# A value product for both halves of the probabilities at once, with VectorE adding the two results

## The chip, the cores and the metric

The kernel runs on one core of a Trainium2 chip. The metric is the device time of one execution in microseconds; the median of three runs is compared.

## The reference

One transformer layer (attention and experts side by side) on x of 32 sequences of 256 tokens with 128 features, all in float32:

```python
xn = _layernorm(x)
# attention: h = relu(xn @ w1 + b1); m = h @ w2 + b2; q, k, v = projections of m
# each query sees the keys at distance -32..32
weights = softmax(where(valid, q . k_band / sqrt(128), -inf))
att = einsum('bsw,bswd->bsd', weights, v_band)
# experts: 16, the best 8 of each token weighted, and one shared expert
y = sum over e of combine[e] * ((silu(xn @ gate[e].T) * (xn @ up[e].T)) @ down[e].T)
x + att + y + shared(xn)
```

## The kernel before, in words

The 32 sequences are worked through in 16 groups of two (512 tokens). Features lie on the partitions and tokens on the free dimension, so that nearly every operation is 128x512. A group has 17 steps (`STEPS`), one for the shared expert and 16 for the experts. Each engine has its own program that walks the same groups and steps (`program`, `slot`), and the order written there is the order of execution on that engine; semaphores tie the engines together. There is no planner.

Every float32 operand of a product is split in two float32r parts, "hi" (the value rounded) and "lo" (the rest), and a product is three matmuls: hi by hi, hi by lo and lo by hi (`PAIRS3`). So wherever a tensor is fed to TensorE, ScalarE writes its hi part from PSUM or SBUF and VectorE subtracts it to get lo.

In slot s of a group TensorE issues `gate_proj` of step s+1 (L466), attention work of this step (`att_early`), `down` of step s-3 (L486, `LAG`), more attention work (`att_late`) and `up_proj` of step s (L476). The other engines handle an expert step like this: ScalarE makes silu of the gate product (L717), GpSimd multiplies it by the routing weight (L1262), VectorE multiplies the up product with it (h_prod, L1134), ScalarE takes the hi part (h_hi, L725) and VectorE the lo part (h_lo, L1140). VectorE's slot s is: h_prod of step s-1, the attention work of the slot (`att`), h_lo of step s-1. The up products alternate between two PSUM banks, so that `up_proj` of step s waits for h_lo of step s-2.

Attention is spread over the steps. The scores of the two sequences are in `bank[2]` and `bank[1]`; mask and row maximum, exp and normalisation follow, and TensorE transposes the probabilities (L437). Each sequence has two blocks of 128 keys, and a block is seen by 160 queries (`WIN`). The hi part of the transposed probabilities is `p_t[0]` (L712), the lo part `p_t[1]` (L1043). The value product `attend` (L447) runs in slots 13 and 14, sequence by sequence, with the hidden state hid_n as the stationary operand: for each key block three matmuls into `bank[2]`, where both sequences have 256 columns each. The first one of a sequence is 256 columns wide (the columns past 160 hold zeros from a memset, L975) so that it writes all columns of the sequence; the other five have 160. The result z is split by `z_hi` (ScalarE, slot 15, L699) and `z_lo` (VectorE, slot 16, L970), and `value_proj` (L456) multiplies it with the value weights at slot 0 of the next group, straight into the bank in which the down products add up.

In VectorE's slot 16, q_lo (L929) of the next group comes behind z_lo and ahead of h_lo. The layer norm's moments of group g+3 (`moments`, four statistics, L828) are in slot 15 and their mean and variance (`variance`, L834 to L845) in slot 0 of the next group. SyncE issues all DMAs in the order of its own slots; x of group g+3 is loaded in slot 3.

Of the kernel before, what the change touches and what calls it, by code (L numbers as in the profile page):

```python
# [72 lines left out]
def layer(nc, x, x_t, watt, watt_t, expert_bias, wexp, out_t, c_dram, st_dram, h_dram):  # L73
    ctx = ExitStack()
    with ctx:
        def sb(name, shape, dt=F32):
            return ctx.enter_context(nc.sbuf_tensor(name, shape, dt))
# [4 lines left out]
        def sem(name):  # L82
# [52 lines left out]


        prob_n = sb("prob_n", [P, NB, 3 * P])
        p_t = [sb("p_hi", [P, NB, 2, SEQ], F32R), sb("p_lo", [P, NB, 2, WIN], F32R)]

# [24 lines left out]
        ps_y = pb("ps_y")  # L166
        bank = [pb(f"bank{i}") for i in range(3)]
        score_bank = [bank[2], bank[1]]


        s_watt_in = sem("watt_loaded")
# [48 lines left out]
            hid_b gate_1 score select top8 rest weight wsum winv comb comb_t  # L220
            hid_mm hid hid_hi hid_lo q_mm q_hi q_lo hid_tp hn_hi hn_lo key_term
            mask_k sc0 sc1 nmax0 nmax1 exp0 exp1 inv0 inv1 pn0 pn1 pt0 pt1
            p0_hi p0_lo p1_hi p1_lo pv z_hi z_lo""".split()
        S = {n: sem(n) for n in names}
        s_hid_st = sem("hid_stored")
        s_hid_m = sem("hid_loaded")
# [13 lines left out]
        def first(g):  # L240
            return g == 0
# [15 lines left out]

        def flat(t):
            return t[:].rearrange("p a d -> p (a d)")

        def windows(b):

            return b[:, 0:2 * APART].rearrange("p (t c) -> p t c", t=2)[:, :, 0:WIN]
# [139 lines left out]
        def _(pe):  # L403
# [36 lines left out]

            def attend(seq):

                for kb in range(2):
                    col = seq * SEQ + kb * (P - HALF)
                    for n, (a, b) in enumerate(PAIRS3):
                        wide = SEQ if kb == 0 and n == 0 else WIN
                        done = mm(bank[2][:, col:col + wide], hid_n[a][:, seq * 2 + kb, :],  # L447
                                  p_t[b][:, seq, kb, 0:wide], start=kb == 0 and n == 0, stop=kb == 1 and n == 2,
                                  skip_group_check=True)
                return done  # L450

            def value_proj(g):
# [158 lines left out]
            def att_late(g, par, s):  # L611

                if s == 0 and not first(g):
                    value_proj(g - 1)
                if s == when(g, 9, 12):
                    pe.wait_ge(S["pn1"], g + 1)
                    turn_probs(1)
                if s == 13:
                    pe.wait_ge(S["hn_lo"], g + 1)
                    pe.wait_ge(S["p0_lo"], g + 1)  # L620
                    attend(0)
                if s == 14:
                    pe.wait_ge(S["p1_lo"], g + 1)
                    attend(1).then_inc(S["pv"], 1)

            def slot(g, par, s):
# [19 lines left out]
                        hid_proj(g + 1, 1 - par)  # L646

            def finish():
                value_proj(GROUPS - 1)
                for s in range(STEPS - LAG, STEPS):  # L650
                    down(GROUPS - 1, (GROUPS - 1) % 2, s)

            program(prologue, slot, finish)

        @block.scalar
        def _(act):
# [39 lines left out]

            def z_hi(g):
                act.wait_ge(S["pv"], g + 1)
                A(z_t[0][:], bank[2][:], ACT.Copy).then_inc(S["z_hi"], 1)  # L699

            def prob_exp(g, seq):
                act.wait_ge(S[f"nmax{seq}"], g + 1)
# [6 lines left out]

            def prob_hi(g, seq):  # L710
                act.wait_ge(S[f"pt{seq}"], g + 1)
                A(p_t[0][:, seq, :, 0:WIN], windows(score_bank[seq]), ACT.Copy).then_inc(S[f"p{seq}_hi"], 1)  # L712

            def gate_silu(g, par, s):
                i = (par + s) % 2
# [101 lines left out]
        def _(dve):  # L817
# [149 lines left out]

            def z_lo(g):
                dve.wait_ge(S["z_hi"], g + 1)
                V.tensor_tensor(z_t[1][:], bank[2][:], z_t[0][:].bitcast(F32), ALU.subtract).then_inc(S["z_lo"], 1)  # L970

            def prologue():
                V.memset(spin_in[:].bitcast(F32), 0.0).then_inc(s_spin, 1)
                V.memset(prob_n[:], 0.0)
                V.memset(p_t[0][:, :, 0, WIN:SEQ].bitcast(F32), 0.0)  # L975
                moments(0, 0)
                variance(0)
                dve.wait_ge(s_gatew_hi, 1)
                V.tensor_tensor(gate_w[:, :, E:2 * E], gate_raw, gate_w[:, :, 0:E].bitcast(F32),
                                ALU.subtract).then_inc(s_gatew, 1)  # L980
                normalise(0, 0)
                xn_lo(0, 0)
                dve.wait_ge(s_attw_hi, 1)
                V.tensor_scalar(vecs[:, 0:1], bank[2][:, M_VEC:M_VEC + 1], att_raw[:, QB:QB + 1], SCALE,
                                ALU.add, ALU.mult)
                V.tensor_scalar(vecs[:, 3:4], bank[2][:, M_VEC + 1:M_VEC + 2], att_raw[:, KB:KB + 1], SCALE,
                                ALU.add, ALU.mult)
                V.tensor_tensor(vecs[:, 1:3], bank[2][:, M_VEC + 1:M_VEC + 3], att_raw[:, KB:VB + 1], ALU.add)\
                    .then_inc(s_vec1, 1)
                V.tensor_tensor(att_w[1][:, 0, :], att_raw[:, W1:W1 + P], att_w[0][:, 0, :].bitcast(F32),  # L990
                                ALU.subtract)
                V.tensor_tensor(att_w[1][:, 2, :], bank[2][:, M_V:M_V + P], att_w[0][:, 2, :].bitcast(F32),
                                ALU.subtract).then_inc(s_attw, 1)
                gate_sum(0)
                route_scores(0)
                route_max(0)
                route_match(0)
                route_sum(0)
                route_weights(0, 0)

                dve.wait_ge(s_side, 1)
                V.tensor_copy(vecs[:, 4:7], ps_u[1][:, M_VEC + 4:M_VEC + 7]).then_inc(s_vec2, 1)
# [37 lines left out]

            def prob_lo(g, seq):
                dve.wait_ge(S[f"p{seq}_hi"], g + 1)
                V.tensor_tensor(p_t[1][:, seq, :, :], windows(score_bank[seq]),  # L1043
                                p_t[0][:, seq, :, 0:WIN].bitcast(F32), ALU.subtract).then_inc(S[f"p{seq}_lo"], 1)

            def att(g, par, s):
                more = not last(g)
                more2 = not last(g, 1)
                if first(g):
                    fresh_att(s)  # L1050
                if s == when(g, 0, 3) and g + 1 < TURNED:
                    normalise(g + 1, 1 - par)
                if s == when(g, 1, 4):
                    hid_n_lo(g)
                if s == when(g, 1, 5):
                    key_terms(g, 0)
                if s == when(g, 2, 5):
                    key_terms(g, 1)
                if s == when(g, 3, 6) and more:
                    xn_lo(g + 1, 1 - par)  # L1060
                if s == when(g, 4, 7):
                    row_max(g, 0)
                if s == when(g, 5, 8) and more:
                    gate_sum(g + 1)
                if s == when(g, 6, 9):
                    normalise_probs(g, 0)
                if s == 7 and more and not first(g):
                    route_scores(g + 1)
                if s == when(g, 8, 11):
                    normalise_probs(g, 1)  # L1070
                if s == when(g, 8, 10) and more:
                    route_max(g + 1)
                if s == when(g, 9, 12):
                    prob_lo(g, 0)
                if s == when(g, 9, 10) and more:
                    route_match(g + 1)
                if s == when(g, 10, 13):
                    prob_lo(g, 1)
                if s == when(g, 10, 11) and more:
                    route_sum(g + 1)  # L1080
                if s == when(g, 11, 12) and more:
                    route_weights(g + 1, 1 - par)
                if g == TURNED - 2:
                    if s == 4:
                        moments(g + 2, par)
                    if s == 5:
                        variance(g + 2)
                if s == 0 and TURNED < g + 2 < GROUPS:
                    variance(g + 2)
                if s == 12 and more:  # L1090
                    hid_blocks(g + 1)
                if s == 13 and first(g):
                    moments(g + 2, par)
                if s == 15 and TURNED < g + 3 < GROUPS:
                    moments(g + 3, 1 - par)
                if s == 14:
                    if first(g):
                        variance(g + 2)
                    if more:
                        hid_lo(g + 1)  # L1100
                if s == 16:
                    z_lo(g)
                    if more:
                        q_lo(g + 1)

            def fresh_att(s):

# [35 lines left out]
            def slot(g, par, s):  # L1143
# [11 lines left out]
                    h_lo(*before(g, par, s))  # L1155
                if first(g) and s == 1:
                    moments(1, 1)
                if first(g) and s == 9:
                    route_scores(1)

# [156 lines left out]
```

## Time and profile before

| | |
|---|---|
| median of 3 runs | 686.98 us (686.58 to 687.01) |
| profiled execution | 687.21 us, span 685.4 us |
| granted TensorE clock | 0.999 of 2.4 GHz |
| TensorE busy | 676.9 us, 3172 matmuls |
| weight loads | 553.8 us |
| VectorE busy | 597.6 us |
| ScalarE busy | 437.2 us |
| GpSimd busy | 443.0 us |

The span runs from the first to the last instruction of the program; the execution has some time around it. Busy time of TensorE counts overlapping matmuls once, and the ends of matmuls are modelled, so the start-to-start distance of two matmuls says more than the duration of one. In the rows, PE is TensorE's matmuls, PEld its weight loads, DVE is VectorE, ACT ScalarE, POOL GpSimd. In what follows "start to start" is the distance between the starts of two instructions that follow each other on an engine; VectorE and ScalarE overlap the end of one with the start of the next by some 0.1 us when nothing has to be waited for.

### The profile page before, as it was taken

The numbers are of one execution on the slowest core, as the hardware profiler recorded it, in microseconds if no ns is written. First come the engines' busy times: TensorE is split into PE (matmuls) and PEld (weight loads), VectorE is DVE, ScalarE is ACT, GpSimd is POOL, SyncE is SP. The second block draws the span as 40 slices with busy tenths as digits, with TensorE's granted clock in tenths as the row PEclk, the third lists the DMA queues.
The fourth block names the chain that finished last, engine by engine and source line by source line (L and its number), as shares of the span: only waits on it lengthen the run. The fifth ranks groups of instructions, "written<-read, shape, count | busy, mean of one in ns | idle before, by whom it ended". The sixth has DMA issues, their size and how long they took to land.

```text
span 685.4 us, 10455 instructions
## 1 busy us (share of the span) xinstructions
PE 676.9 (99%) x3172; PEld 553.8 (81%) x3172; DVE 597.6 (87%) x1640; ACT 437.2 (64%) x874; POOL 443.0 (65%) x400
## 2 busy tenths in 40 slices
PE   7999999999999999999999999999999999999997
PEld 6877788888888888888888888888888888888885
DVE  7998989888889898889888898898889888898775
ACT  5775656657675575666657665575756757666573
POOL 4785666666667756766666667766667567666553
PEclk9999999999999999999999999999999999999999
DMA  8607255252623617155261633617145161631500
GB/s 266 236 9 272 61 186 185 93 232 73 233 113 124 235 46 277 62 173 198 65 260 51 252 116 104 254 45 278 63 163 208 49 262 47 220 121 63 231 0 16
DMA packets 38040, 101.80 MB, mean 149 GB/s; under 512 B 8672, under 2 KB 18144, under 8 KB 29920
## 3 DMA queue, kind: packets, MB, share of 16 engines
q1 hardware_dynamic: 37984, 101.14, 41.1%
q8 instruction: 25, 0.41, 0.2%
q14 instruction: 31, 0.25, 0.1%
HBM read 92.42 MB, written 8.70 MB: 148 GB/s over the span
## 4 chain that ended last, share of the span: by engine, by line
PE 90%; DVE 4%; DMA 3%; ACT 1%; issue 1%; SPq 1%; POOL 0%; DVEq 0%; ACTq 0%
PE ps_y L486 26%; PE ps_u L476 26%; PE ps_g L466 25%; PE bank L408 3%; PE bank L447 3%; PE bank L430 3%; PE bank L437 1%; PE ps_y L456 1%; DMA exp_raw<-wexp 1%; DMA h_dram<-exp_raw 1%; DVE ps_u L1134 1%; PE bank L419 1%; DVE h_lo L1140 1%; DMA exp_raw<-h_dram 0%; DVE prob_n L1037 0%
## 5 line engine op out<-in xcount | busy, mean ns | idle before, releaser
L1262 POOL TENSOR_TENSOR silu_c<-silu,comb_b 128x512 f32<-128x512 f32 x252 | 325.3, 1294 | 220.5 <-ACT silu L717 219.6
L725 ACT ACTIVATE h_hi<-ps_u 128x512 fp32r<-128x512 f32 x272 | 162.9, 599 | 232.9 <-DVE ps_u L1134 232.8
L1140 DVE TENSOR_TENSOR h_lo<-ps_u,h_hi 128x512 fp32r<-128x512 f32 x272 | 186.0, 684 | 37.3 <-ACT h_hi L725 30.4
L1134 DVE TENSOR_TENSOR ps_u<-silu_c,ps_u 128x512 f32<-128x512 f32 x256 | 177.1, 692 | 28.5 <-PE ps_u L476 24.2
L717 ACT ACTIVATE silu<-ps_g 128x512 f32<-128x512 f32 x272 | 162.0, 596 | 0.2
L476 PE MATMUL ps_u<-xn_hi,exp_w_hi 128*128 128x512 f32 x272 | 111.2, 409 | 0.7 <-DVE h_lo L1140 0.6
L486 PE MATMUL ps_y<-h_hi,exp_w_hi 128*128 128x512 f32 x272 | 109.4, 402 | 0.9 <-DVE h_lo L1140 0.4
L466 PE MATMUL ps_g<-xn_hi,exp_w_hi 128*128 128x512 f32 x272 | 108.1, 397 | 1.3 <-ACT silu L717 1.3
L486 PE MATMUL ps_y<-h_lo,exp_w_hi 128*128 128x512 f32 x272 | 107.7, 396 | 0.0
L476 PE MATMUL ps_u<-xn_hi,exp_w_lo 128*128 128x512 f32 x272 | 107.6, 396 | 0.0
L486 PE MATMUL ps_y<-h_hi,exp_w_lo 128*128 128x512 f32 x272 | 107.3, 394 | 0.0
L466 PE MATMUL ps_g<-xn_hi,exp_w_lo 128*128 128x512 f32 x272 | 106.9, 393 | 0.0
L476 PE MATMUL ps_u<-xn_lo,exp_w_hi 128*128 128x512 f32 x272 | 106.7, 392 | 0.0
L466 PE MATMUL ps_g<-xn_lo,exp_w_hi 128*128 128x512 f32 x272 | 105.8, 389 | 0.0
L476 PEld LDWEIGHTS ps_u<-xn_hi,exp_w_hi 128*128 128x128 f32 x272 | 51.2, 188 | 14.0 <-DVE h_lo L1140 3.2
L466 PEld LDWEIGHTS ps_g<-xn_hi,exp_w_hi 128*128 128x128 f32 x272 | 51.0, 188 | 13.9 <-issue 2.0
L486 PEld LDWEIGHTS ps_y<-h_hi,exp_w_lo 128*128 128x128 f32 x272 | 51.3, 189 | 12.2
L476 PEld LDWEIGHTS ps_u<-xn_hi,exp_w_lo 128*128 128x128 f32 x272 | 51.2, 188 | 12.2
L466 PEld LDWEIGHTS ps_g<-xn_lo,exp_w_hi 128*128 128x128 f32 x272 | 51.3, 188 | 12.1
L466 PEld LDWEIGHTS ps_g<-xn_hi,exp_w_lo 128*128 128x128 f32 x272 | 51.0, 188 | 12.3
L486 PEld LDWEIGHTS ps_y<-h_hi,exp_w_hi 128*128 128x128 f32 x272 | 51.2, 188 | 11.2 <-DVE h_lo L1140 0.8
L486 PEld LDWEIGHTS ps_y<-h_lo,exp_w_hi 128*128 128x128 f32 x272 | 51.3, 189 | 9.9
(156 smaller groups left out, 989.2 us busy)
## 6 DMA issues: line engine op xcount, KB each, us to landing
comb_b<-c_dram SPq DMA_DIRECT2D x63, 1024.0 KB, 7.2
mom_b<-st_dram SPq DMA_DIRECT2D x13, 512.0 KB, 3.7
xres<-x_t SPq DMA_DIRECT2D x16, 256.0 KB, 2.6
out_t<-xres SPq DMA_DIRECT2D x16, 256.0 KB, 2.0
xin<-x SPq DMA_DIRECT2D x15, 256.0 KB, 3.2
h_dram<-exp_raw SPq DMA_DIRECT2D x60, 64.0 KB
exp_raw<-h_dram SPq DMA_DIRECT2D x15, 256.0 KB, 3.1
xn<-x_t SPq DMA_DIRECT2D x13, 256.0 KB, 3.3
```

Of the source, the lines that this page charges most:

```text
L408: done = mm(dst[:], att_w[a][:, w, :], parts[b][:], start=n == 0, stop=n == 2)
L419: done = mm(bank[0][:], gate_w[:].rearrange("p q c -> p (q c)"), xn_t[par][n][:], start=n == 0, stop=n == 1)
L430: done = mm(dst[:, t * SEQ:t * SEQ + WIN], q_t[a][:, q0:q0 + P], hid_t[b][:, k0:k0 + WIN], start=n == 0, stop=n == 2)
L447: done = mm(bank[2][:, col:col + wide], hid_n[a][:, seq * 2 + kb, :], p_t[b][:, seq, kb, 0:wide], start=kb == 0 and n == 0, stop=kb == 1 a ...
L466: done = mm(ps_g[i][:], exp_w[a][:, s, 0:P], xn_t[par][b][:], start=n == 0, stop=n == 2)
L476: done = mm(ps_u[i][:], exp_w[a][:, s, P:2 * P], xn_t[par][b][:], start=n == 0, stop=n == 2)
L486: done = mm(ps_y[:], exp_w[a][:, s, 2 * P:3 * P], h_t[i][b][:], start=s == 0 and n == 0, stop=s == STEPS - 1 and n == 2, skip_group_check= ...
L717: A(silu[i][:], ps_g[i][:], ACT.Silu).then_inc(s_silu, 1)
L725: A(h_t[hbuf(par, s)][0][:], ps_u[(par + s) % 2][:], ACT.Copy).then_inc(s_h_hi, 1)
L1134: V.tensor_tensor(ps_u[i][:], src[:], ps_u[i][:], ALU.mult).then_inc(s_h, 1)
L1140: V.tensor_tensor(t[1][:], ps_u[(par + s) % 2][:], t[0][:].bitcast(F32), ALU.subtract)\
L1262: G.tensor_tensor(silu_c[i][:], silu[i][:], comb_b[:, s1 - 1, :], ALU.mult).then_inc(s_silu_c, 1)
```

## The change

The hi and lo parts of the probabilities are put side by side in one tensor `p_t` of [128, 2, 2, 2, 160]: part, sequence, key block, query. Per key block there is one matmul of hid_n_hi with both parts (320 columns, as two runs of 160) and one of hid_n_lo with the hi part (160 columns). The output bank has two halves of 256 columns: the first takes hi by hi and lo by hi, the second hi by lo. So a sequence needs a bank of its own; sequence 0 has `bank[2]`, sequence 1 `bank[0]`, and the second `attend` also waits for hid_hi of the next group, which reads that bank before. `start` is now set on the first matmul alone, and no zeros are needed any more.

z_hi is two operations of 256 columns on the first halves. z_lo is two subtractions of the first halves, a wait for them (`z_rest`), and two additions of the second halves. Three moves come with it: q_lo goes behind h_lo in slot 16; moments go from slot 15 to slot 13 and variance from slot 0 to slot 15; and after the last group `value_proj` comes behind the first of the three last `down`.

```diff
-        p_t = [sb("p_hi", [P, NB, 2, SEQ], F32R), sb("p_lo", [P, NB, 2, WIN], F32R)]
+        p_t = sb("p_t", [P, 2, NB, 2, WIN], F32R)
...
+        att_bank = [bank[2], bank[0]]
...
+        def halves(b):
+            return b[:].rearrange("p (h t) -> p h t", h=2)
...
             def attend(seq):
+                dst = att_bank[seq]
                 for kb in range(2):
-                    col = seq * SEQ + kb * (P - HALF)
-                    for n, (a, b) in enumerate(PAIRS3):
-                        wide = SEQ if kb == 0 and n == 0 else WIN
-                        done = mm(bank[2][:, col:col + wide], hid_n[a][:, seq * 2 + kb, :],
-                                  p_t[b][:, seq, kb, 0:wide], start=kb == 0 and n == 0, stop=kb == 1 and n == 2,
-                                  skip_group_check=True)
+                    c = slice(kb * (P - HALF), kb * (P - HALF) + WIN)
+                    mm(halves(dst)[:, :, c], hid_n[0][:, seq * 2 + kb, :], p_t[:, :, seq, kb, :],
+                       start=kb == 0, stop=False, skip_group_check=True)
+                    done = mm(dst[:, c], hid_n[1][:, seq * 2 + kb, :], p_t[:, 0, seq, kb, :],
+                              start=False, stop=kb == 1, skip_group_check=True)
...
                 if s == 14:
                     pe.wait_ge(S["p1_lo"], g + 1)
+                    pe.wait_ge(S["hid_hi"], g + 1 + (not last(g)))
                     attend(1).then_inc(S["pv"], 1)
...
             def finish():
-                value_proj(GROUPS - 1)
                 for s in range(STEPS - LAG, STEPS):
                     down(GROUPS - 1, (GROUPS - 1) % 2, s)
+                    if s == STEPS - LAG:
+                        value_proj(GROUPS - 1)
...
-                A(z_t[0][:], bank[2][:], ACT.Copy).then_inc(S["z_hi"], 1)
+                for seq in range(NB):
+                    done = A(z_t[0][:, seq * SEQ:(seq + 1) * SEQ], att_bank[seq][:, 0:SEQ], ACT.Copy)
+                done.then_inc(S["z_hi"], 1)
...
             def z_lo(g):
                 dve.wait_ge(S["z_hi"], g + 1)
-                V.tensor_tensor(z_t[1][:], bank[2][:], z_t[0][:].bitcast(F32), ALU.subtract).then_inc(S["z_lo"], 1)
+                for seq in range(NB):
+                    c = slice(seq * SEQ, (seq + 1) * SEQ)
+                    done = V.tensor_tensor(z_t[1][:, c], att_bank[seq][:, 0:SEQ], z_t[0][:, c].bitcast(F32),
+                                           ALU.subtract)
+                done.then_inc(S["z_rest"], 1)
+                dve.wait_ge(S["z_rest"], g + 1)
+                for seq in range(NB):
+                    c = slice(seq * SEQ, (seq + 1) * SEQ)
+                    done = V.tensor_tensor(z_t[1][:, c], att_bank[seq][:, SEQ:2 * SEQ], z_t[1][:, c].bitcast(F32),
+                                           ALU.add)
+                done.then_inc(S["z_lo"], 1)
...
-                V.memset(p_t[0][:, :, 0, WIN:SEQ].bitcast(F32), 0.0)
...
-                if s == 0 and TURNED < g + 2 < GROUPS:
-                    variance(g + 2)
...
+                if s == 13 and TURNED < g + 3 < GROUPS:
+                    moments(g + 3, 1 - par)
                 if s == 15 and TURNED < g + 3 < GROUPS:
-                    moments(g + 3, 1 - par)
+                    variance(g + 3)
...
                 if s == 16:
                     z_lo(g)
-                    if more:
-                        q_lo(g + 1)
...
+                if s == STEPS - 1 and not last(g):
+                    q_lo(g + 1)
```

## Rows read from the trace of the kernel before

**Rows 1.** The page's table: busy us (share of the span), instructions, by engine.

```profile
PE 676.9 (99%) x3172; PEld 553.8 (81%) x3172; DVE 597.6 (87%) x1640; ACT 437.2 (64%) x874; POOL 443.0 (65%) x400
```

**Rows 2.** Waits, 110 to 670 us: who waited for whom, us, times, longest.

```profile
PEld ps_g L466 <- ACT silu L717: 0.2, 1, 0.2
```

**Rows 3.** Waits of the weight loads, 41 to 100 us.

```profile
PEld ps_u L476 <- DVE h_lo L1140: 2.5, 5, 0.7
```

**Rows 4.** Timeline of PE, group 7, slot 13: start us, us, instruction.

```profile
340.81 0.28 PE L447 MATMUL bank<-p_hi,hid_n_hi 128*128 128x256 f32 x1
340.93 0.23 PE L447 MATMUL bank<-p_lo,hid_n_hi 128*128 128x160 f32 x1
341.00 0.28 PE L447 MATMUL bank<-p_hi,hid_n_lo 128*128 128x160 f32 x1
...
341.45 0.43 PE L476 MATMUL ps_u<-xn_hi,exp_w_hi 128*128 128x512 f32 x1
```

**Rows 5.** Timeline of the weight loads, group 7, slot 14.

```profile
343.79 0.19 PEld L447 LDWEIGHTS bank<-p_hi,hid_n_hi 128*128 128x128 f32 x1
343.90 0.19 PEld L447 LDWEIGHTS bank<-p_lo,hid_n_hi 128*128 128x128 f32 x1
```

**Rows 6.** Timeline of PE, group 0: writes with gaps (L514), writes without (L413).

```profile
20.49 0.60 PE L514 MATMUL bank<-ident,comb 128*128 128x128 f32 x4
20.93 0.60 PE L413 MATMUL bank<-ident,hid 128*128 128x128 f32 x4
```

**Rows 7.** Timeline of DVE, group 7, slot 13 to group 8, slot 1.

```profile
341.69 0.69 DVE L1140 TENSOR_TENSOR h_lo<-ps_u,h_hi 128x512 fp32r<-128x512 f32 x1 [0.67 <-ACT h_hi L725]
...
342.98 1.09 DVE L924 TENSOR_TENSOR hid_lo<-hid,hid_hi 128x512 fp32r<-128x512 f32 x1
...
345.74 0.87 DVE L828 BATCH_NORM_STATS2 stats<-xin 128x6 f32<-128x128 f32 x4
...
347.92 0.70 DVE L1134 TENSOR_TENSOR ps_u<-silu_c,ps_u 128x512 f32<-128x512 f32 x1 [0.72 <-PE ps_u L476]
348.52 0.68 DVE L970 TENSOR_TENSOR z_lo<-bank,z_hi 128x512 fp32r<-128x512 f32 x1
...
350.38 0.69 DVE L1134 TENSOR_TENSOR ps_u<-silu_c,ps_u 128x512 f32<-128x512 f32 x1
...
352.78 0.70 DVE L1134 TENSOR_TENSOR ps_u<-silu,ps_u 128x512 f32<-128x512 f32 x1 [0.36 <-PE ps_u L476]
```

**Rows 8.** Timeline of DVE, group 7, slot 10: p_lo of 320 columns, and what follows.

```profile
334.86 0.49 DVE L1043 TENSOR_TENSOR p_lo<-bank,p_hi 128x320 fp32r<-128x320 f32 x1
335.26 0.23 DVE L899 SCALAR_TENSOR_TENSOR weight<-rest,score 128x64 f32<-128x64 f32 x1
335.52 0.22 DVE L902 TENSOR_REDUCE wsum<-weight 128x4 f32<-128x64 f32 x1
```

**Rows 9.** Timeline of ACT, group 7, slot 15.

```profile
346.83 0.61 ACT L699 ACTIVATE z_hi<-bank 128x512 fp32r<-128x512 f32 x1
```

**Rows 10.** Timeline of DVE, group 8: h_prod of step 4.

```profile
362.26 0.70 DVE L1134 TENSOR_TENSOR ps_u<-silu_c,ps_u 128x512 f32<-128x512 f32 x1 [0.41 <-PE ps_u L476]
```

**Rows 11.** Timeline of DVE, group 7: h_lo of step 7.

```profile
331.51 0.68 DVE L1140 TENSOR_TENSOR h_lo<-ps_u,h_hi 128x512 fp32r<-128x512 f32 x1
```

**Rows 12.** Timeline of PE: up products of step 9 (group 7) and step 2 (group 8).

```profile
332.40 0.48 PE L476 MATMUL ps_u<-xn_hi,exp_w_hi 128*128 128x512 f32 x1
...
356.06 0.40 PE L476 MATMUL ps_u<-xn_hi,exp_w_hi 128*128 128x512 f32 x1
```

**Rows 13.** Timeline of ACT, group 1, slot 0.

```profile
62.35 0.63 ACT L695 ACTIVATE hid_n_hi<-exp_raw 128x512 fp32r<-128x512 f32 x1 [2.01 <-DMA exp_raw<-h_dram]
```

**Rows 14.** Timeline of DVE, group 15, slot 16.

```profile
677.10 0.70 DVE L1134 TENSOR_TENSOR ps_u<-silu_c,ps_u 128x512 f32<-128x512 f32 x1
...
678.46 0.69 DVE L1140 TENSOR_TENSOR h_lo<-ps_u,h_hi 128x512 fp32r<-128x512 f32 x1
```

**Rows 15.** Timeline of PE, the last down product.

```profile
681.16 0.50 PE L486 MATMUL ps_y<-h_hi,exp_w_hi 128*128 128x512 f32 x1 [0.37 <-DVE h_lo L1140]
```

More of the change, by code:

```diff
@@ L222, in layer @@
             mask_k sc0 sc1 nmax0 nmax1 exp0 exp1 inv0 inv1 pn0 pn1 pt0 pt1
-            p0_hi p0_lo p1_hi p1_lo pv z_hi z_lo""".split()
+            p0_hi p0_lo p1_hi p1_lo pv z_hi z_rest z_lo""".split()
         S = {n: sem(n) for n in names}
@@ L711, in prob_hi @@
                 act.wait_ge(S[f"pt{seq}"], g + 1)
-                A(p_t[0][:, seq, :, 0:WIN], windows(score_bank[seq]), ACT.Copy).then_inc(S[f"p{seq}_hi"], 1)
+                A(p_t[:, 0, seq, :, :], windows(score_bank[seq]), ACT.Copy).then_inc(S[f"p{seq}_hi"], 1)
             def gate_silu(g, par, s):
@@ L1042, in prob_lo @@
                 dve.wait_ge(S[f"p{seq}_hi"], g + 1)
-                V.tensor_tensor(p_t[1][:, seq, :, :], windows(score_bank[seq]),
-                                p_t[0][:, seq, :, 0:WIN].bitcast(F32), ALU.subtract).then_inc(S[f"p{seq}_lo"], 1)
+                V.tensor_tensor(p_t[:, 1, seq, :, :], windows(score_bank[seq]),
+                                p_t[:, 0, seq, :, :].bitcast(F32), ALU.subtract).then_inc(S[f"p{seq}_lo"], 1)
             def att(g, par, s):
```

## The prediction

> **What bounds the kernel now.** I read the engine table first. TensorE is busy for 99% of the span, VectorE for 87%, ScalarE and GpSimd for two thirds [rows 1]. A busy TensorE is no proof (the ends of its matmuls are modelled), so the list of waits came next: from 110 to 670 us TensorE waits for nobody but for 0.2 us [rows 2]; the five other waits for h_lo that matter, 2.5 us, fall into 41 to 100 us, in groups 0 and 1, where VectorE still carries the start-up work [rows 3]. So from group 2 on the time is the sum of TensorE's start-to-start intervals, and whatever shortens these shortens the run, as long as VectorE, whose h_lo releases the up product two steps later, keeps pace. The timelines then give both: the price of a value product, and VectorE's reserve.
>
> **The value products, before.** Six matmuls per sequence: 256 columns, then five of 160. From the first (340.81) to the next up product (341.45) it is 0.64 us [rows 4]. The intervals are not columns alone: after the 256-column product comes 0.12, then 0.07, and then 0.11 again and again. Weight loads start 0.11 apart [rows 5], so a 160-column product (0.067 us of columns at the granted 2.4 GHz) is paced by the weight load behind it, unless a longer product ahead has let the loads run ahead; then its interval is 0.07. Were the block one of a stage with TensorE waits, none of this would count; [rows 2] exclude that.
>
> **After.** Four matmuls: 320, 160, 320, 160. By the same pattern: 320 columns are 0.133 us plus the 0.01 that the 256-column product took above its 0.107, so 0.145; the 160 behind it 0.075, its successor's load having started with it; then the load after that comes at 0.255, inside the second 320, which ends its interval at 0.365; the last 160 ends at 0.44. So 0.64 - 0.44 = 0.195 us a sequence, 0.39 a group. Bounds: if every 160 costs its full 0.11 and each 320 0.15, the block is 0.52 and gives 0.115; with bare columns, 960 at 2.4 GHz, it is 0.40 and gives 0.235. I take 0.195, because the row nearest to the new pair (256 then 160) shows just this.
>
> The new operand and output are two runs of 160 with a gap. The trace has one kind of PE write with a gap, the transposes of L514 (four runs of 32): four of them take 0.60 us, as four contiguous ones of L413 do [rows 6]. The Trainium skill speaks against it ("PSUM — Partial Sum Buffer", Specifications (TRN2)): an access pattern that is not contiguous slows matmuls significantly; these rows don't agree, but they are weight-paced and short, so the rule is a rival below. The Trainium skill's page "TensorE: Matmul & The Clock Gate" (Back-to-back issue gap) puts the gap at N/2.4 + 2.5 ns; by that the block would be 0.41 us and the run 0.9 us shorter than I forecast, but for a 160-column product it gives 69 ns, where [rows 4, 5] show 110 for most.
>
> **VectorE and ScalarE.** z_lo goes from one 512-column operation (0.60 start to start, as h_prod ahead of it, 347.92 to 348.52) to four of 256 with a wait in between. A 320-column operation out of PSUM takes 0.40 start to start, a 512 one 0.60 [rows 7, 8], so 256 takes 0.33. An operation that needs the one before starts 0.03 after its end (335.52 against 335.26 + 0.23), not 0.09 ahead of it: 0.12 more. Sum 4 x 0.33 + 0.12 = 1.44, so +0.84 us. Bounds: below, the time of two 512-column operations (1.20: no fixed part for the extra instructions, no wait) gives +0.60; above, half of hid_lo's 1.02 for 512 columns (342.98, both operands in SBUF) for each of the four, and the 0.12, gives 2.1, so +1.5. I take +0.84: the PSUM rows are the nearest, and z_lo reads PSUM. Queued behind it on VectorE are h_lo(15), q_lo and the next h_prod, and TensorE's up product waits for h_lo(15). ScalarE's z_hi becomes two operations, some 0.2 us more; it ends at 347.4 [rows 9], less 0.4 plus 0.2, long before 348.1.
>
> Moments at step 13: four statistics, 0.87 us, fall into the 0.67 us in which VectorE waits for ScalarE at 341.69 [rows 7]; the 0.2 that sticks out is gone in the idle time before h_prod(15), 0.72. Without that cover they would delay h_lo(12) by 0.9, and TensorE's up(14) by what its slack doesn't hold. x landed long ago, its load is issued in step 3. Variance at step 15 is six small instructions; were each as dear as one statistic (0.22), 1.3 instead of 0.87 us stand ahead of h_lo(14), and the 0.4 more fits into the same 0.72. At step 0 it leaves a hole and no gain: an h_lo with nothing ahead of it still starts 1.36 after h_prod (0.69, and 0.67 idle for h_hi at 341.69). q_lo behind h_lo(15) frees h_lo by q_lo's length; nobody needs q_lo before step 3. The new wait for hid_hi is met three steps earlier. The memset removed (0.2 us) is in the start, beside the load of x. All nothing.
>
> **Does VectorE keep pace?** Shifting [rows 7] by -0.39: h_prod 347.53, z_lo 348.13 to 349.57; z_lo, q_lo and h_lo took 1.86 (348.52 to 350.38) and take 2.70, so h_prod is at 350.83 (it was 350.38), h_lo at 352.19 behind h_hi, and the next h_prod at 352.80 where TensorE would allow 352.39. So 0.41 late. From there VectorE has no idle time until h_prod(4), before which it idled 0.41, or 0.49 by start-to-start [rows 10]. The lateness is gone there, with 0.08 left, and behind it, in steps 9 to 12, there is one more cushion: h_lo ends at 332.19, the up product that needs it starts at 332.40 [rows 11, 12]. Together 0.28 us of reserve. In between, the tightest is up(2) (356.06, then 355.67), whose h_lo(0) now ends near 355.33: 0.3 left, no wait.
>
> **Start and tail.** The 0.39 of group 0 is lost: in group 1, step 0, ScalarE waits 2.0 us for the hidden state's DMA, whose issue doesn't depend on steps 13 to 16, and TensorE then waits for VectorE [rows 3, 13]; the later h_prod hides in the same wait. At the end VectorE is the path: h_prod(15) 677.10, h_lo(15) 678.46, h_prod(16), h_lo(16), and the last down product at 681.16 waits for it [rows 14, 15]. There z_lo's +0.84 shows, less 0.16 that h_lo(15) waited for h_hi (677.10 and two operations of 0.60 are 678.30): +0.68. That value_proj moves behind down(14) costs nothing and hides the later z_lo.
>
> **Sum.** 15 groups x 0.39 = 5.85, less 0.68: 5.2 us. The profiled execution took 687.21 (span 685.4 and 1.8 around it), 0.23 over the median of 686.98: 682.0 by the one, **681.8** by the other. A change under 0.2%, 1.4 us, can't be told from none.
>
> **Rivals.**
> A. Weight loads pace all 160-column products: block 0.52. The first rows speak against (0.07 after the 256). Sum 15 x 0.23 - 0.68 = 2.8: 684.2.
> B. VectorE doesn't keep pace. It decides once z_lo's four cost over 1.44 + 0.28 = 1.72 us: from there each group loses the excess, as a TensorE wait for h_lo in steps 9 to 12. At the upper bound (2.1) that is 0.38, just the gain: 0 for the groups, and the tail +1.3: 688.3. Half of it: about 685. For it: reserve of 0.28 in 41 us. Against: durations out of PSUM agree across three lines.
> C. Slower: the product with gaps streams at half rate, 0.27 for 320 columns. Block 0.28 + 0.075, twice: 0.71, +0.075 x 30 = 2.3, + 0.68: 690.0. It decides from 0.24 us per 320-column product, where the block is 0.64 again. Against it: four writes with gaps at full pace [rows 6]. For it: the Trainium skill's rule above.
> D. The change doesn't do what it says for TensorE: the block shrinks by what the up product behind it grows, since its weights load no sooner. Then only the tail's 0.68 is left, 687.6. For it: the load behind the last 160 is not ahead; against: nor is it today, behind five of them.
>
> **Chances.** Forecast 0.70, A 0.12, B 0.08 (half of it still faster), C 0.05, D 0.05. Faster 0.87: forecast, A and over half of B; same 0.06: D and a little of B; slower 0.07: C and the rest of B. Range 680.3 (bare columns: 15 x 0.47 - 0.68 = 6.4) to 684.8, beyond A; the forecast's own is 681.0 to 682.8.
>
> **What would show it.** Right: 320-column products with 0.14 to 0.15 to the next start, 160 ones 0.075; blocks of 0.44; z_lo block 1.4 to 1.5; VectorE's idle before h_prod(4) down from 0.41 to under 0.1; groups of 40.95; a last down product near 676.0. Wrong: TensorE waits for h_lo in steps 9 to 12 of groups after 2 (B), intervals over 0.24 behind a 320 (C), 0.11 behind each 160 (A).

## The result and the profile after

The changed kernel takes 708.51 us (median of 4 runs, 708.44 to 709.19) against 687.0 of the kernel before on the same chip: ratio 1.0315, 95% interval 1.0297 to 1.0333. It is slower by 21.5 us; 5.2 us faster were forecast. The profiled execution has a span of 707.4 us and a granted clock of 1.00.

| | before | after |
|---|---|---|
| span | 685.4 us | 707.4 us |
| TensorE busy | 676.9 (99%) | 678.7 (96%) |
| VectorE busy | 597.6 (87%) | 630.8 (89%) |
| ScalarE, GpSimd busy | 437.2, 443.0 | 438.4, 442.8 |
| one group (start of its first gate product to the next one's) | 41.35 | 42.86 |

VectorE has 33 us more busy time, yet the two subtractions and two additions of a group add only 0.86 x 16 = 14 us. The page's table and chain of the changed kernel, to be read beside [rows 1]:

```profile
PE 678.7 (96%) x3108; PEld 548.0 (77%) x3108; DVE 630.8 (89%) x1687; ACT 438.4 (62%) x890; POOL 442.8 (63%) x400
...
PE 62%; DVE 22%; issue 5%; ACT 5%; DMA 4%; POOL 1%; SPq 1%; DVEq 0%; ACTq 0%
```

The waits of TensorE's weight loads, 110 to 690 us, where the kernel before had 0.2 us from 110 to 670 [rows 2] (us in total, times, longest):

```profile
PEld ps_u L484 <- DVE h_lo L1160: 18.9, 13, 1.5
...
PEld ps_y L494 <- DVE xres L1036: 6.8, 14, 0.5
```

So in each group TensorE waits twice. The timeline of PE, group 8, shows where: the up product of step 2 and the down product that opens the new group's sum in slot 3:

```profile
366.41 0.50 PE L484 MATMUL ps_u<-xn_hi,exp_w_hi 128*128 128x512 f32 x1 [1.02 <-DVE h_lo L1160]
...
369.03 0.50 PE L494 MATMUL ps_y<-h_hi,exp_w_hi 128*128 128x512 f32 x1 [0.33 <-DVE xres L1036]
```

Put slot by slot (from one gate product to the next, median over ten groups), after less before: the interval with the up product of step 2 +1.29 us, the one with the down product of step 0 +0.56, the two with the value products -0.16 and -0.17, the next -0.01, all others within 0.01. Sum +1.51, and 42.86 - 41.35 is 1.51. The whole loss stands in two places, and the value products do give a gain.

The value products themselves, PE's timeline of the changed kernel, beside [rows 4]:

```profile
350.31 0.31 PE L454 MATMUL bank<-p_t,hid_n_hi 128*128 128x320 f32 x1
350.45 0.23 PE L456 MATMUL bank<-p_t,hid_n_lo 128*128 128x160 f32 x1
350.52 0.35 PE L454 MATMUL bank<-p_t,hid_n_hi 128*128 128x320 f32 x1
350.71 0.24 PE L456 MATMUL bank<-p_t,hid_n_lo 128*128 128x160 f32 x1
350.78 0.44 PE L484 MATMUL ps_u<-xn_hi,exp_w_hi 128*128 128x512 f32 x1
```

Intervals 0.15, 0.07, 0.19 and 0.07 (by the unrounded starts, the median of all blocks from group 2 on): 0.477 us where 0.634 was.

Now VectorE, from slot 16 of group 7 to slot 3 of group 8; [rows 7] have the first part of it for the kernel before. The two kernels are best compared by the distance to the first gate product of group 8, which starts here in the kernel before and in the changed one:

```profile
347.72 0.40 PE L466 MATMUL ps_g<-xn_hi,exp_w_hi 128*128 128x512 f32 x1
```

```profile
356.88 0.40 PE L474 MATMUL ps_g<-xn_hi,exp_w_hi 128*128 128x512 f32 x1
```

VectorE of the changed kernel:

```profile
357.68 0.75 DVE L985 TENSOR_TENSOR z_lo<-bank,z_hi 128x256 fp32r<-128x256 f32 x2
358.47 0.76 DVE L991 TENSOR_TENSOR z_lo<-bank,z_lo 128x256 fp32r<-128x256 f32 x2
359.14 0.68 DVE L1160 TENSOR_TENSOR h_lo<-ps_u,h_hi 128x512 fp32r<-128x512 f32 x1
...
360.39 0.69 DVE L1154 TENSOR_TENSOR ps_u<-silu_c,ps_u 128x512 f32<-128x512 f32 x1
...
362.35 0.69 DVE L1154 TENSOR_TENSOR ps_u<-silu,ps_u 128x512 f32<-128x512 f32 x1
362.95 1.24 DVE L962 TENSOR_TENSOR hid_n_lo<-exp_raw,hid_n_hi 128x512 fp32r<-128x512 f32 x1
364.11 0.34 DVE L975 CUSTOM_DVE_ANT_0 key_prod<-exp_raw,key_row,vecs 128x128 f32<-128x128 f32 x1
...
364.38 1.36 DVE L975 CUSTOM_DVE_ANT_0 key_prod<-exp_raw,key_row,vecs 128x128 f32<-128x128 f32 x1
...
365.67 0.68 DVE L1160 TENSOR_TENSOR h_lo<-ps_u,h_hi 128x512 fp32r<-128x512 f32 x1
...
368.23 0.74 DVE L1036 SCALAR_TENSOR_TENSOR xres<-ps_y,vecs,xres 128x512 f32<-128x512 f32 x1
```

z_lo takes 1.46 (357.68 to 359.14). h_prod(0), the row at 362.35, starts 5.47 behind the group's first gate product, and 5.06 in the kernel before, where it waited for TensorE: it is 0.41 late. Both are as forecast. Then two instructions that the change doesn't touch are much longer: hid_n_lo 1.24 and the second key_prod 1.36 us, where its twin right ahead of it takes 0.34. GpSimd at that time, its products of steps 1 and 2:

```profile
362.35 1.29 POOL L1284 TENSOR_TENSOR silu_c<-silu,comb_b 128x512 f32<-128x512 f32 x1 [2.71 <-ACT silu L730]
364.24 1.36 POOL L1284 TENSOR_TENSOR silu_c<-silu,comb_b 128x512 f32<-128x512 f32 x1 [0.60 <-ACT silu L730]
```

hid_n_lo (362.95 to 364.19) ends 0.55 after the first of them ends (363.64). The second key_prod begins 0.14 after the second product started and ends (365.74) 0.14 after that one's end (365.60). In the kernel before, the same four instructions all but went past each other. Its GpSimd:

```profile
352.33 1.30 POOL L1262 TENSOR_TENSOR silu_c<-silu,comb_b 128x512 f32<-128x512 f32 x1 [1.87 <-ACT silu L717]
354.68 1.29 POOL L1262 TENSOR_TENSOR silu_c<-silu,comb_b 128x512 f32<-128x512 f32 x1 [1.06 <-ACT silu L717]
```

and its VectorE:

```profile
353.39 0.78 DVE L949 TENSOR_TENSOR hid_n_lo<-exp_raw,hid_n_hi 128x512 fp32r<-128x512 f32 x1
354.10 0.34 DVE L962 CUSTOM_DVE_ANT_0 key_prod<-exp_raw,key_row,vecs 128x128 f32<-128x128 f32 x1
...
354.37 0.34 DVE L962 CUSTOM_DVE_ANT_0 key_prod<-exp_raw,key_row,vecs 128x128 f32<-128x128 f32 x1
```

There the first product of GpSimd ended at 353.63, 0.24 into hid_n_lo (0.78 us; it has 0.68 in experiment 3, where that product is cut short), and the second key_prod started 0.31 before the second product. That 0.31 was the margin of the kernel before, and no row that the prediction cites shows it.

GpSimd's products are late too, and the first of them by more than VectorE: it starts 5.47 behind the group's first gate product instead of 4.61, so 0.86 late, where hid_n_lo is 0.40 late. ScalarE passes this on, in the kernel before and in the changed one:

```profile
351.10 0.60 ACT L725 ACTIVATE h_hi<-ps_u 128x512 fp32r<-128x512 f32 x1 [1.36 <-DVE ps_u L1134]
351.59 0.59 ACT L717 ACTIVATE silu<-ps_g 128x512 f32<-128x512 f32 x1
```

```profile
361.12 0.60 ACT L738 ACTIVATE h_hi<-ps_u 128x512 fp32r<-128x512 f32 x1 [2.22 <-DVE ps_u L1154]
361.61 0.59 ACT L730 ACTIVATE silu<-ps_g 128x512 f32<-128x512 f32 x1
```

VectorE's h_prod(16) of group 7, the first thing behind slot 16's work, is late by all that was added ahead of it (360.39 here, 350.38 in [rows 7]; 3.51 against 2.66 from the gate product). ScalarE's h_hi(16) waits for it, silu of step 1 stands behind h_hi(16), and GpSimd's product of step 1 waits for this silu.

What hid_n_lo and key_prod have in common: they take both operands from SBUF, all others in the fence of VectorE after have one in PSUM, and GpSimd reads SBUF. The Trainium skill ("SBUF — State Buffer", Who interferes with whom) says that a VectorE instruction with two SBUF inputs contends with a GpSimd one that reads SBUF, that such contention is an exclusive lock, and that the order of issue decides which of the two is blocked. The trace agrees in that the one issued second was held. It doesn't show it held from its very start: hid_n_lo ends 0.55 behind GpSimd's end and key_prod 0.14 behind, both less than the 0.68 and 0.34 that they take alone.

### The profile page after: what moved, and what is told of

Same layout as the page of the kernel before. It is cut to its first block, busy times and chain, and to the rows that moved or that the text cites. A ratio compares the mean times of both kernels' runs of the same rounds, so it can differ in the third digit from the quotient of the medians.

```text
span 707.4 us, 10406 instructions
## 1 busy us (share of the span) xinstructions
PE 678.7 (96%) x3108; PEld 548.0 (77%) x3108; DVE 630.8 (89%) x1687; ACT 438.4 (62%) x890; POOL 442.8 (63%) x400
## 4 chain that ended last, share of the span: by engine, by line
PE 62%; DVE 22%; issue 5%; ACT 5%; DMA 4%; POOL 1%; SPq 1%; DVEq 0%; ACTq 0%
PE ps_y L494 19%; PE ps_u L484 18%; PE ps_g L474 17%; DVE ps_u L1154 6%; DVE h_lo L1160 3%; DVE key_prod L975 3%; PE bank L416 3%; ACT h_hi L738 3%; DMA h_dram<-exp_raw 2%; DVE xres L1036 2%; DVE hid_n_lo L962 1%; PE bank L438 1%; DVE z_lo L985 1%; PE bank L454 1%; PE bank L445 1%
## 5 line engine op out<-in xcount | busy, mean ns | idle before, releaser
L484 PE MATMUL ps_u<-xn_hi,exp_w_hi 128*128 128x512 f32 x272 | 112.7, 414 | 15.1 <-DVE h_lo L1160 15.1
```

Of the source, the lines that this page charges most:

```text
L484: done = mm(ps_u[i][:], exp_w[a][:, s, P:2 * P], xn_t[par][b][:], start=n == 0, stop=n == 2)
```

## The experiments

Theory P, as it was put ahead of the runs: VectorE, late at h_prod(0) (0.44 us, as the expectations have it; 0.41 by the rows above), drives hid_n_lo and key_prod into GpSimd's products, and is then late for two waits of TensorE. Experiment 9 sets right how the lateness gets there. Its rivals: L, VectorE has too much work; T, the new matmuls, banks or the wait for hid_hi; M, the three moves.

**1. q_lo to where variance was** (label x1_qlo_slot0). All work kept, only its place changed:

```diff
                 if s == when(g, 0, 3) and g + 1 < TURNED:
                     normalise(g + 1, 1 - par)
+                if s == 0 and not first(g):
+                    q_lo(g)
...
-                if s == STEPS - 1 and not last(g):
-                    q_lo(g + 1)
```

> The changed kernel with one move more: VectorE's q_lo stands in slot 0 of the next group, ahead of h_lo(16), where variance used to be, instead of behind h_lo(15). All work is kept. Theory P (lockout): VectorE reaches h_prod(0) 0.44 us late, GpSimd's products of steps 1 and 2 then run into hid_n_lo and key_prod, whose operands are both in SBUF, and each waits until the other is done. With q_lo moved h_prod(0) is on time again, hid_n_lo is back at 0.8 us, both key_prod at 0.34, groups take 41.05 and the run 683 us. Theory L (load): VectorE simply has 0.84 us a group too much to do; the work is the same, so 705 to 709 us. Theory T (TensorE: the new operands, banks and the wait for hid_hi): 708.

Measured: 685.34 us, ratio 0.9974 (0.9964 to 0.9983) to the kernel before. key_prod is back at 0.343 us mean, hid_n_lo at 0.94. Nothing was taken from VectorE's work and 23 us are gone: L and T fall. Groups take 41.20, though, not 41.05, and hid_n_lo isn't back at 0.8: h_prod(16) is still 0.20 late, and by the way over ScalarE so is GpSimd's product of step 1, which holds it longer, while h_prod(0) and the start of hid_n_lo are in time.

**2. Without the additions** (x2_no_adds): the second loop of z_lo and its wait left out, and with them the products in the second halves of the banks.

> The changed kernel without the two additions and the wait ahead of them; the product of the hi part of the probabilities with the lo part of hid is thus left out of the result. Theories P and L: VectorE is on time at h_prod(0); the matmuls' gain of 2 x 0.158 us a group stays: 41.03 a group, 682.5 us. Theory T: over 700.

Measured: 685.38 us, groups 41.15 to 41.19, key_prod 0.342, hid_n_lo 0.92. The changed matmuls alone don't cost anything. But the size is off by 2.9 us, as it was by 2.3 in 1: there is a second, smaller loss that isn't the additions'. (1.6 us of the 2.9 are in group 2, which took 42.78 here and has both waits of the changed kernel, 1.20 and 0.56; why it alone has them stays open.)

**3 and 4. GpSimd's product of one step cut short** (x5_narrow1, x6_narrow2). The other 448 of its 512 columns are left out of the result. The diff is that of x5; x6 has step 2 in the place of 1. VectorE's program is untouched, and h_prod(0) is as late as in the changed kernel:

```diff
-                    G.tensor_tensor(silu_c[i][:], silu[i][:], comb_b[:, s1 - 1, :], ALU.mult).then_inc(s_silu_c, 1)
+                    w = 64 if s1 in (1,) and not first(g1) else T
+                    G.tensor_tensor(silu_c[i][:, 0:w], silu[i][:, 0:w], comb_b[:, s1 - 1, 0:w], ALU.mult).then_inc(s_silu_c, 1)
```

> The changed kernel, with GpSimd's product of step 1 cut to 64 of 512 columns in groups 1 to 15 (the rest of that product is left out); VectorE's own work and order are untouched. Theory P: hid_n_lo (1.19 us) falls to about 0.7, and key_prod behind it is through before GpSimd's product of step 2 starts, so it falls from 0.58 to 0.34 though nothing of step 2 was touched. h_prod(0) stays 0.4 late; its end product xres is then 0.25 late for the down product of step 0. Groups 41.3, the run 686 to 688 us. Theory L: 705 to 709, GpSimd's load doesn't matter. Theory T: 708.

Measured: 686.52 us, groups 41.30, hid_n_lo 0.685 mean, key_prod 0.355. VectorE of this run:

```profile
352.20 0.69 DVE L1154 TENSOR_TENSOR ps_u<-silu,ps_u 128x512 f32<-128x512 f32 x1
352.80 0.68 DVE L962 TENSOR_TENSOR hid_n_lo<-exp_raw,hid_n_hi 128x512 fp32r<-128x512 f32 x1
353.40 0.34 DVE L975 CUSTOM_DVE_ANT_0 key_prod<-exp_raw,key_row,vecs 128x128 f32<-128x128 f32 x1
...
353.67 0.35 DVE L975 CUSTOM_DVE_ANT_0 key_prod<-exp_raw,key_row,vecs 128x128 f32<-128x128 f32 x1
```

and its GpSimd:

```profile
352.19 0.33 POOL L1285 TENSOR_TENSOR silu_c<-silu,comb_b 128x64 f32<-128x64 f32 x1 [2.71 <-ACT silu L730]
354.09 1.29 POOL L1285 TENSOR_TENSOR silu_c<-silu,comb_b 128x512 f32<-128x512 f32 x1 [1.56 <-ACT silu L730]
```

The product of step 2 is whole and where it was in the changed kernel, counted from the gate product; the second key_prod (353.67) now starts 0.42 ahead of it, because hid_n_lo didn't have to wait. Cutting one GpSimd instruction of a group gives back 22 us.

> As the one before, with GpSimd's product of step 2 cut instead of that of step 1. Theory P: hid_n_lo stays at 1.19, the second key_prod falls from 1.36 to 0.34 us; xres is 0.7 late for the down product of step 0: groups 41.7, the run 692 to 696 us. Theories L and T: 705 to 709.

Measured: 694.74 us, groups 41.88. VectorE:

```profile
356.32 1.24 DVE L962 TENSOR_TENSOR hid_n_lo<-exp_raw,hid_n_hi 128x512 fp32r<-128x512 f32 x1
...
357.75 0.40 DVE L975 CUSTOM_DVE_ANT_0 key_prod<-exp_raw,key_row,vecs 128x128 f32<-128x128 f32 x1
```

hid_n_lo keeps its 1.24, key_prod is free. hid_n_lo's time thus hangs on GpSimd's product of step 1, and the second key_prod's on that of step 2 once hid_n_lo is late. Both times and both durations came as expected: that these two collisions make the loss is shown.

**5. The second edge** (x8_both_moves). Slot by slot, x1 has lost 0.18 us in the interval with the down product of step 0, which xres releases. In the kernel before, xres ended at 357.94 and the weight load of that down product started at 358.01:

```profile
357.20 0.74 DVE L1014 SCALAR_TENSOR_TENSOR xres<-ps_y,vecs,xres 128x512 f32<-128x512 f32 x1
```

```profile
358.01 0.19 PEld L486 LDWEIGHTS ps_y<-h_hi,exp_w_hi 128*128 128x128 f32 x1
```

Counted from the gate product, xres ends 0.21 later in x1 (hid_n_lo took 0.99 there and 0.78 before), and 0.18 are lost: the slack was 0.03. So xres goes ahead of h_lo(1), which waits for h_hi there anyhow:

```diff
-                if s == 3 and not first(g):
-                    finish_group(g - 1, 1 - par)
...
                 att(g, par, s)
+                if s == 2 and not first(g):
+                    finish_group(g - 1, 1 - par)
                 if some:
                     h_lo(*before(g, par, s))
```

> q_lo in slot 0 as in x1_qlo_slot0, and VectorE's xres (finish_group, the end product of the group before) one place earlier, in slot 2 ahead of h_lo(1) instead of at the head of slot 3. In x1 the groups take 41.20 and not 41.03: the down product of step 0 starts 0.18 us later relative to its neighbours, by VectorE's xres, which hid_n_lo's longer duration (0.94 against 0.78) makes late. Theory P with this second edge: the 0.18 goes, groups 41.03, the run 682.5 to 683. Theory L, or a TensorE loss spread over the group: 685.3 as x1.

Measured: 682.39 us (682.23 to 682.89), ratio 0.9928 (0.9914 to 0.9941): faster than both kernels. Groups 41.02; slot by slot only the value products' two differ from the kernel before, by -0.16 and -0.17. VectorE of this kernel:

```profile
348.31 0.75 DVE L942 SCALAR_TENSOR_TENSOR q_lo<-bank,vecs,q_hi 128x512 fp32r<-128x512 f32 x1
...
349.93 0.70 DVE L1156 TENSOR_TENSOR ps_u<-silu,ps_u 128x512 f32<-128x512 f32 x1 [0.17 <-PE ps_u L484]
350.53 0.99 DVE L962 TENSOR_TENSOR hid_n_lo<-exp_raw,hid_n_hi 128x512 fp32r<-128x512 f32 x1
...
351.71 0.34 DVE L975 CUSTOM_DVE_ANT_0 key_prod<-exp_raw,key_row,vecs 128x128 f32<-128x128 f32 x1
...
353.73 0.74 DVE L1036 SCALAR_TENSOR_TENSOR xres<-ps_y,vecs,xres 128x512 f32<-128x512 f32 x1
```

h_prod(0) waits for TensorE again, and the second key_prod starts 0.11 before GpSimd's product of step 2 (351.82). That is a thinner margin than the 0.31 of before.

**6. The same move alone in the kernel before** (x9_before_early).

> The kernel before, with xres (finish_group) in slot 2 ahead of h_lo(1), as in x8_both_moves, and nothing else. TensorE waits for nobody in the groups of the kernel before, so all theories say no change: groups 41.34, 687 us. If it were faster by 2 us or more, x8's gain would be this move's and not the value products'.

Measured: 686.82 us, ratio 0.9994 (0.9985 to 1.0004). No change: x8's gain is the value products', let through.

**7. The same move alone in the changed kernel** (x10_after_early).

> The changed kernel with xres in slot 2 ahead of h_lo(1), and nothing else. Of the 1.85 us a group that TensorE waits in the changed kernel 0.56 stand at the down product of step 0 (released by xres) and 1.29 at the up product of step 2 (released by h_lo(0)). Theory P: the first goes, the second stays: groups 42.3, the run 699 to 701 us, key_prod and hid_n_lo as long as before the move.

Measured: 700.47 us. The 8 us of the down product go, the rest stays.

**8 and 9. Doses of VectorE work in the kernel before** (x7a_dose128, x7c_dose384). The matmuls are the old ones:

```diff
             def z_lo(g):
                 dve.wait_ge(S["z_hi"], g + 1)
+                V.tensor_tensor(extra[:, 0:128], bank[2][:, 0:128], z_t[0][:, 0:128].bitcast(F32), ALU.subtract)
```

> The kernel before (its value products untouched), with one operation more in VectorE's slot 16: a subtraction of 128 columns into a spare tile, 0.19 us start to start. Theory P: hid_n_lo starts as before, ends 0.19 later, and the second key_prod still starts before GpSimd's product of step 2: key_prod stays 0.34; xres is 0.1 late for the down product. Groups 41.45, the run 688.5. Theory L: the same or less.

Measured: 689.74 us, groups 41.52, key_prod 0.344, hid_n_lo 0.97. The 0.17 is all at the down product that xres releases. It is dearer than expected. h_prod(0) and hid_n_lo start in time, but h_prod(16) and with it GpSimd's product of step 1 are 0.20 late, so that hid_n_lo takes longer, and xres ends 0.21 late and not 0.1.

> As the one before with 384 columns, 0.46 us. Theory P: the second key_prod would start after GpSimd's product of step 2 and waits for its end: key_prod's mean over 0.55, its second one 1.3 us; groups 42.6 to 42.7, the run 705 to 708, so over 1.2 us a group for 0.46 us of work. Theory L: at most the work itself, 0.46 a group, under 694.

Measured: 708.34 us, groups 42.81, key_prod 0.582, hid_n_lo 1.20. The group's first gate product, then VectorE:

```profile
356.83 0.40 PE L467 MATMUL ps_g<-xn_hi,exp_w_hi 128*128 128x512 f32 x1
```

```profile
357.64 0.55 DVE L971 TENSOR_TENSOR extra<-bank,z_hi 128x384 f32<-128x384 f32 x1
...
359.96 0.69 DVE L1136 TENSOR_TENSOR ps_u<-silu_c,ps_u 128x512 f32<-128x512 f32 x1
...
361.93 0.69 DVE L1136 TENSOR_TENSOR ps_u<-silu,ps_u 128x512 f32<-128x512 f32 x1
362.52 1.24 DVE L950 TENSOR_TENSOR hid_n_lo<-exp_raw,hid_n_hi 128x512 fp32r<-128x512 f32 x1
...
363.95 1.37 DVE L963 CUSTOM_DVE_ANT_0 key_prod<-exp_raw,key_row,vecs 128x128 f32<-128x128 f32 x1
```

0.19 us of work costs 0.17 a group, 0.46 costs 1.47: a step, not a slope. Under L no dose can cost more than itself. It also shows that 0.46 us in slot 16, without any change of the matmuls, makes the kernel before as slow as the changed one.

And it sets Theory P right. h_prod(0), the row at 361.93, is all but in time here: 5.09 us behind the gate product against 5.07 in the kernel before (medians of groups 4 to 14). Both collisions are there all the same. What is late is h_prod(16), the row at 359.96, by 0.47, and GpSimd with it; its ScalarE and its GpSimd:

```profile
360.68 0.60 ACT L726 ACTIVATE h_hi<-ps_u 128x512 fp32r<-128x512 f32 x1 [1.83 <-DVE ps_u L1136]
361.18 0.59 ACT L718 ACTIVATE silu<-ps_g 128x512 f32<-128x512 f32 x1
```

```profile
361.91 1.30 POOL L1264 TENSOR_TENSOR silu_c<-silu,comb_b 128x512 f32<-128x512 f32 x1 [2.32 <-ACT silu L718]
363.81 1.36 POOL L1264 TENSOR_TENSOR silu_c<-silu,comb_b 128x512 f32<-128x512 f32 x1 [0.60 <-ACT silu L718]
```

So it isn't VectorE that comes late to GpSimd's first product but this product that comes late to hid_n_lo. In all kernels of this case in which it is whole, hid_n_lo ends 0.55 after it (medians of the same groups), wherever hid_n_lo itself starts. The second key_prod follows behind it, and collides once it is pushed back by over 0.31 us (the margin) more than GpSimd's second product is: the smaller dose pushes it back by 0.21, this one would by 0.47. In the changed kernel the lateness of h_prod(0) comes on top of this (1.29 lost at the up product of step 2 instead of 0.91).

**10. The three moves undone** (x3_moves_undone).

> The changed kernel with its three moves on VectorE undone: moments in slot 15, variance in slot 0, q_lo ahead of h_lo(15). Theory P: h_prod(0) is as late as with the moves, since variance fits into the idle time ahead of h_lo(16); key_prod and hid_n_lo as long as in the changed kernel, 707 to 710 us. Theory M (the moves are at fault): 683 to 688.

Measured: 708.91 us, groups 42.87, key_prod 0.579, hid_n_lo 1.20. The moves of q_lo, moments and variance, as the change makes them, neither cost nor help; M falls. (q_lo in slot 0, as in 1, is another place than either kernel has.)

Of these, 1, 5 and 6 were timed in rounds. The others are one execution each and are read by their groups, which from group 3 on agree within 0.04 us in each; the smallest effect read so, experiment 8's, is 0.17 us a group.

## Why the prediction was wrong

**Bound of the kernel before**: right. TensorE waits for nobody from group 2 on, and what shortens its intervals shortens the run, one for one (x8).

**The value products**: mechanism right, size off. 0.477 us a sequence instead of the forecast 0.44, so 0.157 gained and not 0.195. The first pair is as forecast (0.147 and 0.070); the second 320-column product's interval is 0.187, not 0.145. Its weight load starts 0.07 ahead of it and the first one's 0.23 (350.45 and 350.08), which fits the prediction's own reading of the 160-column products that took 0.11; that this is the reason isn't shown. As to the formula N/2.4 + 2.5 ns, the Trainium skill's page ("TensorE: Matmul & The Clock Gate", Back-to-back issue gap) gives it for an isolated matmul and adds that at small N it gives too little beside weight loads; the 0.11 of [rows 4, 5] agree with that addition. The gap in operand and output costs nothing that shows, by the first product of 320: of rival C nothing came, and here the measurement speaks against the general form of the Trainium skill's sentence in "PSUM — Partial Sum Buffer" (Specifications (TRN2)) that a non-contiguous pattern slows matmuls significantly. Two runs of 160 don't.

**z_lo**: right, 1.46 us against 1.44. ScalarE's z_hi, the moments, variance, q_lo where the change puts it, the wait for hid_hi: no cost, as said (x3 for the moves, x8 for the others).

**"So 0.41 late"**: right, 0.41. That h_prod(16) is then 0.84 late (350.83, where 349.99 would be in time) is in the sum too (0.86 measured), but it was not followed to ScalarE and GpSimd.

**The step that failed**: "From there VectorE has no idle time until h_prod(4) [...] The lateness is gone there, with 0.08 left". It carries the lateness along VectorE alone, through slots 0 to 4, with the durations that VectorE's instructions had in the kernel before, and puts GpSimd at nothing. But two of them, hid_n_lo and the second key_prod, don't have a duration of their own: they take as long as GpSimd's instruction beside them lets them. And the 0.86 us of h_prod(16) reach GpSimd's product of step 1 over ScalarE in full. Between h_prod(0) and h_lo(0) this cost 1.46 us more, 3.32 (362.35 to 365.67) instead of 1.86 (352.78 to 354.64). Rival B had the right engine and the right kind of wait, and a wrong place and threshold: it was to decide at 1.72 us for z_lo, in steps 9 to 12. The doses put that of the collisions between 0.79 and 1.06 (0.60 and the dose), and the wait stands in steps 2 and 0.

**A second miss in the same step**: "In between, the tightest is up(2)". Up(2) had 0.6 us (in x6 h_lo(0) ends 0.92 late, counted from the gate product, and 0.32 are lost). Far tighter was the down product of step 0 behind xres, with 0.03. x5, in which the collisions are taken away and the lateness is kept, shows what this costs: xres ends 0.30 late and 0.28 are lost, so that groups take 41.30 instead of 41.02 and the run 686.5 us. So even without the collisions the change as made would have been next to no gain.

**The end**: right. From h_prod(15) of the last group to the end of xres it is 5.83 us in the kernel before and 6.51 in the changed one and in x8: the forecast +0.68. In x2, without the additions, it is 5.83.

**The start**: that group 0 gives nothing can't be read from these runs. Group 2 starts at 99.64 us in the kernel before, 99.74 in the changed one and 98.76 in x8, but at 99.31 in x9 too, which has the old value products.

**Sum**: with the two moves of VectorE's work 5.1 us are there, where 5.2 were forecast, but that they meet so closely is in part luck. In the spans of the profiled executions (685.4 and 680.6), groups 2 to 15 give 14 x 0.33 = 4.6, the end takes 0.7, and 0.9 stands in groups 0 and 1, where nothing was forecast. The change as made lacks the two moves and pays 1.29 and 0.56 us a group. The lower end of the range has a slip: 6.4 us under 687.0 is 680.6 and not 680.3.

## What to carry to other kernels

Before a lateness is carried through an engine's timeline with the old durations, look at what GpSimd does beside each VectorE instruction with both operands in SBUF: such a pair that just misses each other is a cliff, and its margin (here 0.31 us) belongs in the sum beside the slack of the waits. Carry the lateness through the other engines as well: here the 0.86 us of one VectorE instruction came back over ScalarE and GpSimd, while VectorE itself had made up half of it. List the slack of every wait that the delayed engine releases, the seldom ones too, and count it to the weight load: the once-a-group xres had 0.03 us where h_lo(0) had 0.6. And when work has to be added to a nearly full engine, look for a hole in the same engine's order first: variance had left one of 0.67 us in slot 0, and moving q_lo into it was worth 23 us.

## What the runs showed of the hardware

A VectorE instruction of 128x128 with both operands in SBUF took 1.36 us instead of 0.34 when GpSimd had started a 128x512 product 0.14 us earlier, and one of 128x512 took 1.24 instead of 0.68 when the product had started 0.60 earlier. The second one ended 0.55 us after GpSimd's product whether the two had overlapped for 0.24 us (kernel before) or 0.69 (changed kernel). The other way round GpSimd lost far less: its product took 1.36 to 1.40 instead of 1.29 when key_prod had started 0.11 to 0.15 earlier.

TensorE's interval behind a matmul depends on its neighbours: a 160-column product had 0.07 behind a 320-column one and 0.11 behind another of its size, and a 320-column one had 0.15 behind a 512 and 0.19 behind a 160.
